# A hybrid block on one core: squares of y shared between two engine pairs, a new step order and another ending

## The reference, cut to what matters

```python
x = x + attn_a(layernorm(x), ...)      # u, B, C projections; rotation; scan over time; rmsnorm(y) @ out_proj
x = x + ffn(layernorm(x), ...)         # einsum with a ternary weight, plus bias
x = x + attn_b(layernorm(x), ...)      # softmax over the 8 rows at each time step
x = x + ffn(layernorm(x), ...)

def rmsnorm(y, w):                     # inside attn_a, over the 512 inner features
    return y * rsqrt(mean(y * y, axis=-1) + EPS) * w
```

## Time and profile before

| what | us |
|---|---|
| median of 3 runs | 598.55 |
| lowest and highest | 597.16 and 598.97 |
| the profiled execution, its own time | 597.6 |
| the span of its trace | 595.8 |

### The profile page before, as it was taken

The page is one execution under the profiler, slowest core; times in us unless marked ns, Lnnn a source line. Parts: engine busy times, 40 slices in busy tenths (PEclk is TensorE's granted clock), DMA queues, the critical chain, the costliest instruction groups (busy, mean ns, idle before and its releaser), DMA issues. The chain is left out here.

```text
span 595.8 us, 12817 instructions
## 1 busy us (share of the span) xinstructions
PE 521.4 (88%) x3932; PEld 435.3 (73%) x3932; DVE 470.9 (79%) x1093; ACT 479.9 (81%) x1477; POOL 433.6 (73%) x568
## 2 busy tenths in 40 slices
PE   4979999999999889899999898999999787879187
PEld 4867888888887777688887777788777665756085
DVE  5665577677767999997758999997559999954994
ACT  3799999999998987789998869699999889853101
POOL 7447777888778696977778786877768886954742
PEclk9989999999999999999999999999999999998669
DMA  8832122222111111133211121232211211000001
GB/s 191 234 101 64 59 77 98 60 81 89 49 59 61 60 50 35 61 95 96 60 38 59 61 61 54 66 96 95 72 50 39 69 62 65 21 19 2 0 1 36
DMA packets 52302, 39.35 MB, mean 66 GB/s; under 512 B 7302, under 2 KB 48011, under 8 KB 52235
## 3 DMA queue, kind: packets, MB, share of 16 engines
q1 hardware_dynamic: 45898, 35.39, 20.2%
q10 hardware_dynamic: 6336, 3.15, 1.8%
HBM read 33.44 MB, written 4.46 MB: 64 GB/s over the span
## 5 line engine op out<-in xcount | busy, mean ns | idle before, releaser
L937 ACT ACTIVATE turned<-ps,sct 128x128 f32<-128x128 f32 x376 | 110.2, 446 | 0.0
L922 ACT ACTIVATE turned<-ps,sct 128x128 f32<-128x128 f32 x368 | 102.9, 433 | 5.1 <-issue 4.3
L1282 DVE TENSOR_TENSOR_SCAN lmat<-arow,band 128x512 f32<-128x512 f32 x64 | 86.0, 1349 | 3.6 <-POOL band L651 3.6
L630 POOL TENSOR_TENSOR cn<-turned 128x256 f32<-128x256 f32 x64 | 54.9, 858 | 39.9 <-ACT turned L937 39.9
L1816 PE MATMUL ps<-cT,bT 128*128 128x128 f32 x512 | 71.4, 283 | 8.6 <-DVE state L1321 6.3
L1290 DVE TENSOR_TENSOR mmat<-ps,lmat 128x512 f32<-128x512 f32 x64 | 43.9, 686 | 44.0 <-PE ps L1816 43.8
L1816 PEld LDWEIGHTS ps<-cT,bT 128*128 128x128 f32 x512 | 64.1, 193 | 15.7 <-issue 14.5
L630 POOL TENSOR_TENSOR bn<-turned 128x256 f32<-128x256 f32 x64 | 51.9, 811 | 28.5 <-PE ps L1848 16.9
L828 ACT ACTIVATE area<-ps 128x256 f32<-128x256 f32 (+1 forms) x68 | 34.8, 568 | 39.9 <-PE ps L2049 14.3
L1721 PE MATMUL ps<-w_sel_hi,xt_hi 128*128 128x512 f32 x128 | 59.5, 465 | 1.6 <-ACT turned L937 1.6
L1848 PE MATMUL ps<-wu,bn 128*128 128x128 f32 x384 | 53.7, 283 | 3.5 <-DVE mmat L1290 3.4
(11 more groups left out here) (272 smaller groups left out, 1408.3 us busy)
## 6 DMA issues: line engine op xcount, KB each, us to landing
arow<-alpha_rows SPq DMA_DIRECT2D x32, 512.0 KB, 3.8
drow<-decay_rows SPq DMA_DIRECT2D x64, 128.0 KB, 3.0
area<-in_L_attn_a_x_dram SPq DMA_DIRECT2D x4, 512.0 KB, 6.6
xT_rows<-turned SPq DMA_DIRECT2D x4, 512.0 KB, 5.4
xt<-xT_rows SPq DMA_DIRECT2D x32, 64.0 KB, 2.5
area<-in_L_attn_a_x_dram ACTq DMA_DIRECT2D x6, 256.0 KB, 3.1
out_dram<-area ACTq DMA_DIRECT2D x6, 256.0 KB, 2.5
area<-L_attn_a_sel_proj_w_dram SPq DMA_DIRECT2D x2, 512.0 KB, 6.8
```

The source lines that it names most:

```text
L630: pool.tensor_tensor(out[:, 0], zc[:, 0], zs[:, 1], ALU.subtract)
L922: last = act.activation(dst[h][:, N * q:N * q + N], bank(BK_B)[:, N * q:N * q + N], ACT.Copy, scale=scalars(c, k)[:, at + HH * h + q:at + ...
L937: last = act.activation(dst[h][:, N * q:N * q + N], bank(BK_C)[:, N * q:N * q + N], ACT.Copy, scale=scalars(c, k)[:, at + HH * h + q:at + ...
L1282: dve.tensor_tensor_scan(lmat[h], arow[i2][:, HH * P * h:HH * P * (h + 1)], band[h], 0.0, ALU.mult, ALU.add).then_inc(l_dve, 1)
```

## The change

It has five parts.

1. **Squares.** `squares_on_pe(tile)` is true in tiles 3 to 6 of chunks 1 to 3. There ACT squares `yT` with its blocks side by side into one of two buffers, DVE does nothing, and PE sums with four one-column matmuls in place of one. In the 20 other tiles ACT does nothing: DVE multiplies yT by itself into the interleaved buffer, waits for its own result, and sums as before.
2. **Step order.** The order within a step is written anew. On PE, ACT and DVE the cycle of the main steps is nearly the same; on POOL `weigh_u` moves behind the next band, and `add_c` of odd units ahead of it. `weigh_u` and `state_of` wait for the chunk's scalars in every step. The positions in `PLACE` move, most of them by less than a step.
3. **Head pieces.** In the last chunk those of pairs 0 to 2 move up: turns, feed-forward and keys of pair 0, and turn and feed-forward of pair 1 stand before the scores and turns of units 14 and 15, and further pieces before the last `project_out`.
4. **Values again.** ACT evacuates the values of the last chunk twice, the second time in the order (head, d, row) into `vals_er`, once the DMAs that read that area are done.
5. **Ending.** Rows 4 to 7 use `vals_er`, so that DVE sums over the eight rows by four reductions (`sum_values`) in place of four folds, and PE turns one tile per row in place of adding 8 or 2. POOL folds rows 2 and 3 once. PSUM banks are dealt out differently, the order of the norms and last products is changed, and PE gets products that nobody reads (`keep_warm`) at seven places.

Core of the diff:

```diff
+SQUARES_ON_PE = (3, 4, 5, 6)
+def squares_on_pe(tile):
+    return tile >= NB and tile % NB in SQUARES_ON_PE
...
             def y_square(c, b):
                 tile = NB * c + b
+                if not squares_on_pe(tile):
+                    return
                 act.wait_ge(y_dve, 2 * tile + 2)
-                after(act, q_dve, tile)
-                act.activation(ysq[:].rearrange("p (t j) -> p j t", j=4), yT[b % 2].rearrange("p (j t) -> p j t", j=4),
-                               ACT.Square).then_inc(ysq_act, 1)
+                after(act, o_pe, tile - 1)
+                act.activation(ysq_both[:, b % 2], yT[b % 2], ACT.Square).then_inc(ysq_act, 1)
...
             def y_sum(c, b):
                 tile = NB * c + b
-                dve.wait_ge(ysq_act, tile + 1)
+                if squares_on_pe(tile):
+                    return
+                own, n = ysq_both[:, b % 2], sums_done(tile, False)
+                dve.wait_ge(y_dve, 2 * tile + 2)
+                after(dve, o_pe, tile - 1)
+                y = yT[b % 2].rearrange("p (j t) -> p j t", j=4)
+                dve.tensor_tensor(own.rearrange("p (t j) -> p j t", j=4), y, y, ALU.mult).then_inc(yq_dve, 1)
+                dve.wait_ge(yq_dve, n)
                 after(dve, o_pe, tile)
...
             def project_out(c, b, more):
-                pe.wait_ge(q_dve, tile + 1)
+                if squares_on_pe(tile):
+                    pe.wait_ge(ysq_act, sums_done(tile, True))
+                else:
+                    pe.wait_ge(q_dve, sums_done(tile, False))
...
-                pe.matmul(bank(BK_M)[:, D:D + 1], ysum[:], ones[:, 0:1], start=True, stop=True).then_inc(o_pe, 1)
+                if squares_on_pe(tile):
+                    for j in range(4):
+                        last = pe.matmul(bank(BK_M)[:, D:D + 1], ysq_both[:, b % 2, P * j:P * j + P], ones[:, 0:1], start=(j == 0), stop=(j == 3))
+                else:
+                    last = pe.matmul(bank(BK_M)[:, D:D + 1], ysum[:], ones[:, 0:1], start=True, stop=True)
...
-PLACE = {"hrms:0": 10.75, "hx1:0": 10.786, "rr:0": 11.296, "hroot0:0": 11.407, "hnorm0:0": 11.441,
+PLACE = {"hrms:0": 6.444, "hroot0:0": 6.667, "hx1:0": 6.773, "hrms:1": 9.714, "hnorm0:0": 9.854,
...
             def f_hvals(c, p):
-                evac(vals_last[:, pair(p), :], kv_bank[p].rearrange("p (s e) -> p s e", s=2)[:, :, D:2 * D]).then_inc(ha[p], 1)
+                rows = kv_bank[p].rearrange("p (s e) -> p s e", s=2)[:, :, D:2 * D]
+                evac(vals_last[:, pair(p), :], rows)
+                for g in range(2):
+                    act.wait_ge(rows_free[g], 16 * NC)
+                evac(vals_er[:, :, pair(p)].rearrange("p e s -> p s e"), rows).then_inc(ha[p], 1)
...
-            fold(6, 512, "v", "a")
-            fold(7, 512, "v", "a")
-            fold(6, 256, "a", "h")
-            fold(7, 256, "a", "h")
+            sum_values(4)
+            sum_values(5)
+            sum_values(6)
             attended(0)
+            sum_values(7)
             attended(1)
...
+            def turn_row(p, s):
+                pe.wait_ge(tv, TV["r", s])
+                at = P * (s % 2)
+                return pe.transpose(acc_bank[p][:, at:at + P], xn[:, s], ident[:])
...
-            add_rows(1, 2, NB)
-            end_tick(add_rows(1, 3, NB), ("acc", 1))
+            add_rows(1, 2, NB // 2)
+            end_tick(add_rows(1, 3, NB // 2), ("acc", 1))
```

279 lines of the change are left out of this document (151 added, 128 removed), and 70 rows, old and new, of tables (PLACE, TV).

## The result

The changed kernel is slower: 610.18 us (median of 4 runs, 609.19 to 611.56) against 598.69 us for the kernel before beside it. The ratio is 1.0204, with a 95% interval of 1.0175 to 1.0234. I had forecast 588.5 us, a range of 581.5 to 596.5, and 0.07 for slower. The trace's span grew from 595.8 to 608.7 us, 12.9 us.

A forecast was written before the change was run, and what follows sets the result against it. ScalarE was taken to bound chunk 0 with TensorE close behind, later stages TensorE, VectorE or ScalarE. Terms -2.6 - 2.1 - 0.9 + 1.0 - 3.7 - 1.8 = -10.1 us gave 587.5 from 597.6, stated as 588.5 on the median's scale, range 581.5 to 596.5.

The forecast's parts named there:

- Squares in chunk 0: Chunk 0: moving squares from ScalarE to VectorE shortens tiles towards TensorE's bound, -2.6 us (bounds -4.5 and +3.5).
- Squares in the stages that VectorE bounds: VectorE-bound stages of three chunks: sums removed, squares added at 0.60 us each, -0.9 us (-2 to +5).
- Rival (a): Squares block VectorE and GpSimd, each taking 1.89 us: about 601.7 us, slower than before; chance 0.07 in full, milder form 0.13.
- Sums on TensorE: Tiles 3 to 6: removed VectorE sums save 1.20 us a chunk; TensorE's added records cost +1.0 us (0 to +2).
- The stages that ScalarE or TensorE bounds: Later chunks: relieving ScalarE gives -0.3 each in chunks 1 and 2, -1.5 in the last chunk's first stage; -2.1 us.
- Order of the steps: All steps: GpSimd's later weighing of u is covered, shifted pieces even out; 0, with 2 us either way.
- Head pieces: End of last chunk: 7.0 us leave the stretch behind the last tile, a 3.3 us stall comes before it; net -3.7.
- Rival (b): Head pieces give nothing, as TensorE's stall before units 14 and 15 equals the saving: 592.1 us; chance 0.20 shared with another rival.
- Ending: After the last chunk: reductions replace folds and waits for TensorE shrink, -1.8 us (+1 to -4).
- rival (c): Whole kernel: everything off the path gains in full, in chunk 0, head and ending: about 583.5 us; chance 0.20.

The follow-up runs named there:

- experiment 1: Kernel before plus the squares part alone, at the old places in the old step order: 609.58 us, ratio 1.0189.
- experiment 5: Kernel before plus the squares part alone, with VectorE's squares written contiguously and its sums reading across the blocks: 608.18 us, ratio 1.0172.
- Experiment 9: Kernel before with contiguous squares on VectorE in the 8 tiles of chunk 0 only: 598.23 against 597.25 us, ratio 1.0015.
- experiment 6: Kernel before plus the squares part and GpSimd's new step order, table and other engines as before: 646.17 us (2 runs), ratio 1.0816.
- Experiment 13: Kernel before plus the squares part, except that tiles 1 and 2 of chunks 1 to 3 stay as before: 597.60 against 597.60 us, ratio 1.0005.
- Experiment 10: Kernel before with only tiles 3 to 6 of chunks 1 to 3 squared contiguously on ScalarE and summed on TensorE: 596.79 against 597.25 us, ratio 0.9993.
- experiment 2: Changed kernel with the old squares in all tiles but the last, whose square stays on VectorE: 610.19 us, ratio 1.0195.
- experiment 11: Kernel before, old squares and steps, with the new positions of the attention pieces alone: 622.75 us, ratio 1.0427.
- experiment 8: Changed kernel with the last chunk's head pieces at their old positions in the table: 611.97 us, ratio 1.0246.
- experiment 3: Kernel before with the new ending alone, squares, step order and places as before: 597.42 against 597.38 us, ratio 0.9995.

## Why the prediction was wrong, point by point

Two steps carry the miss. The order of the steps was put at 0 without a reason and lost 9.9 us before the last chunk; and a square in the stretches that VectorE bounds was priced at 0.60 us on VectorE alone, where two of them cost 4 to 5 us a chunk.

**Squares in chunk 0: -2.6 forecast; +2.5 measured for the whole change, -0.1 for the squares alone** (experiment 1). Three steps of the term failed. First, the undisturbed price of the square was taken from a product of two contiguous tiles, 0.69 us; with the interleaved write it is 1.07 us, and experiment 5 shows that the interleaving is the reason and that whichever instruction crosses the blocks pays it. My total of 1.10 us is near the measured median of 1.14 only by luck, because I had added the disturbance to a base that was too low; beside GpSimd it is 1.58, and 2.02 at the longest. Second, I measured the cover where TensorE's outputs wait for the weighing (0.33 us) and overlooked the scores, which wait for the state update behind the square. Experiment 9, where nearly all is as favourable as it can be, shows what then is left of the gain: 0.3 us in the trace for the whole chunk, and nothing in the time. Third, GpSimd's new order puts a band in front of the square; experiment 6 gives it about half of the loss in chunk 0. That ScalarE was full was right, but TensorE's own work (11.54 of 11.83 us) and the chain over VectorE's state update stood only 0.3 us behind it.

**Squares in the stages that VectorE bounds: -0.9 forecast; +4 to +5 a chunk in experiment 1.** The bound of +5 that I gave for this term is for all three chunks; it was a third of what came (13.5 us). The steps that failed are the price of a square (0.60 us of shift for each; it was 1.1 and 1.6) and that I priced VectorE alone. Its delay made TensorE wait 2.06 us, TensorE's clock fell, and the slower scores gave VectorE a wait that it had not had. Rival (a) had the mechanism and the place, squares of tiles 1 and 2, and put it at 2.4 us a chunk and a chance of 0.07 in full. With its own price of up to 1.89 us a square it gave 601.7. Experiment 13 shows that these six squares are the whole loss of this part.

**Sums on TensorE.** The forecast for the removed sums of tiles 3 and 4 was 1.2 us a chunk, 3.6 in all, and +1.0 for the added records. Experiment 10 has these two parts alone: 2.5 us given and 2.2 taken in its trace, nothing in the time. The gain was put too large and the price too small.

**The stages that ScalarE or TensorE bounds: -2.1 forecast.** In the last chunk's first stage, where I gave 1.5 us to ScalarE's relief, the distance of units 1 to 4 shrank by 0.3 us in experiments 1 and 13, and the milestone of unit 1 had come 0.4 us later. As in chunk 0, ScalarE's full row was not worth its price.

**Order of the steps: 0 forecast, with 2 us either way; 9.9 us measured without the squares** (experiment 2, up to unit 1 of the last chunk). This is the largest failure. I checked one moved instruction, the weighing of u, found 5 us of cover, and took the shifted pieces as even without a reason. Moving attention pieces inside a stretch in which VectorE has 0.6 us of slack in 33.5 cost 8 us a chunk in experiment 11, a mixture of old steps and new positions, so that this is no measure of the changed kernel's own part. I had named the order as what would make me wrong most, but gave it 2 us and no rival. Why the new order loses where it does stays open.

**Head pieces: -3.7 forecast; +1.8 measured for the two stretches (+5.9 and -4.1), not all of it theirs.** Of the 7.0 us that were to go behind the last tile, 4.1 went (20.9 us are left, forecast 18). Ahead of it I had counted only a wait of 3.3 us, and TensorE's moved products as nothing. They arrive as work: between units 12 and 14 TensorE is busy 17.94 us against 12.48 before, and against 13.48 with the old positions (experiment 8). But these 4.5 us of work don't explain the stretch, which is 20.15 us long, 18.49 with the old positions and 14.05 before: 4.4 of the 6.1 us are there without them. The rows of the changed kernel:

```profile
529.28 1.91 PE L1859 MATMUL ps<-cT,bT 128*128 128x128 f32 x8
530.85 0.77 PE L1764 MATMUL ps<-w_sel_hi,xt_hi 128*128 128x512 f32 x1
531.42 0.63 PE L1765 MATMUL ps<-w_sel_lo,xt_hi 128*128 128x512 f32 x1
...
533.01 0.44 PE L1985 MATMUL ps<-ident,small 128*128 128x128 f32 x2 [0.47 <-ACT small L855]
533.92 0.28 PE L1991 MATMUL ps<-bias,ones 3*128 3x256 bf16 x1 [0.48 <-ACT small L855]
```

The scores at 529.28 take 1.91 us where they take 1.06 to 1.13 at full clock; the granted clock over units 12 to 14 is 0.92, before 1.00. Rival (b), the head pieces give nothing, fits the sum of the two stretches, but by experiment 8 they give 2.0 us within the new steps. What they give alone no run shows.

**Ending: -1.8 forecast, -1.4 measured in the changed kernel, no gain shown** (experiment 3). The folds, the reductions and the wait of 0.93 us for GpSimd's product (0.8 forecast) came as worked out:

```profile
592.66 1.22 DVE L1646 TENSOR_REDUCE area<-area 128x128 f32<-128x1024 f32 x1 [0.93 <-POOL area L821]
```

But of the waits that the term takes away, 1.10 us and 2.1 of 3.08, some 2 us were no property of the old ending. In experiment 13, with the old ending and TensorE's clock up earlier, the first is gone and the second is 2.11; from the first scores to the end that kernel takes 35.9 us, and the changed one 36.6. So the nearness of -1.4 to -1.8 is luck: the step that failed is that waits of one trace at a low clock were priced as waits of the order of instructions.

**The parts don't add.** The squares alone cost 12 us, the change without the squares 13 us, all together 11.5 us. Both press on the same VectorE-bound units, so that each may fill waits that the other makes; this isn't shown, and how it comes about stays open.

**Two slips in the working.** For rival (c) its terms give 588.5 - 0.9 - 2.3 - 1.2 = 584.1, not 583.5. And between 1.10 us (-10.1) and 1.89 us (+3.2) for a square the sum passes 0 at 1.7, not 1.6. Neither touches the forecast.

## What to carry to other kernels

An instruction that moves to another engine must be priced at its exact access pattern and at every stage that it will stand in: six of twenty squares stood in a stretch without slack, and they were the whole loss of that part. An engine that is 100% busy is worth relieving only by the distance to the next bound, and that distance has to be taken at every instruction of the next engine that waits for the helper, here the scores behind the state update as well as the outputs. Work that is moved up has to be added where it arrives; and an order written out by hand (or by a planner) and its steps are one fitted thing, so a new one is not even just because its pieces are the same. And a wait that stands in one trace at a low clock is not yet a gain for whoever removes it: the same kernel code may show it shorter in the next.

## What the runs showed of the hardware

A VectorE product of two SBUF tiles of 128x512 that writes with a stride of four elements took 1.07 us, and 0.68 us when it wrote contiguously; the sum over the same tile took 1.07 us when it read across the blocks and 0.69 when it did not. The total is nearly the same either way, 1.76 and 1.75 us.

Such a product, or a scan with two SBUF inputs, took longer when a GpSimd instruction was running as it started (square 1.58 in place of 1.07, scan up to 2.35 in place of 1.22 us) and ended after it, and the next GpSimd instruction took longer in turn (0.62 us became 1.35). The busy time of both engines contains this: 22.2 us more on GpSimd for the same 568 instructions in experiment 1.

TensorE's granted clock fell from 1.00 to 0.73 in the six microseconds that contained and followed a wait of 2.06 us in the middle of the pipeline, and a turn of four records that takes 0.60 us took 1.06. Over units 4 to 8 the same 231 records took 2.8 us longer than before. In the ending the same 48 records of TensorE took 7.75 us in one kernel and 5.62 in another, with a granted clock of 0.69 and 1.00 in the window beside them.
